# One kernel, a linear attention, an NF4 feed-forward network, an autocorrelation and a linear layer: the autocorrelation's weights transformed at plain delays, its output built from even and odd parts, and the neighbouring linear layer's steps put in another order

## What is computed

```python
x = x + tanh(g_xattn[0]) * linear_attention(layernorm(x), ctx, ctx)
x = x + tanh(g_ffn[0])   * nf4_ffn(layernorm(x), ...)
x = x + tanh(g_xattn[1]) * autocorrelation(layernorm(x), ctx, ctx)
x = x + tanh(g_ffn[1])   * dora_linear(layernorm(x), W, lora_A, lora_B, magnitude)

# autocorrelation, for each batch and channel over the 256 positions t:
corr = ifft(fft(q) * conj(fft(k))).real          # 256 delays
w, idx = top_k(corr, 11); w = softmax(w)
out[t] = sum_i w[i] * v[min(idx[i] + t, 255)]
```

## Time and profile before

| | |
|---|---|
| time, median of 3 runs | 2123.46 us (2122.21 to 2124.3) |
| the profiled execution's own time | 2125.07 us |
| its span in the profile | 2123.3 us |
| TensorE busy | 2036.6 us (96% of the span) |
| VectorE, ScalarE, GpSimd busy | 1098.1, 1175.8, 665.0 us |
| mean granted TensorE clock | 0.986 |
| start of the tail phase's loop | about 1608 us, so some 515 us of the span |

### The profile page before, as it was taken

One profiled execution on the slowest core, in us unless ns is written; L12 is line 12 of the kernel. 1 busy time (PEld: TensorE's weight loads), 2 busy tenths in 40 slices (PEclk: granted clock), 3 DMA queues, 4 the chain that ended last, 5 costly groups with the idle time before them and its releaser, 6 DMA issues. The chain is left out here.

```text
span 2123.3 us, 25966 instructions
## 1 busy us (share of the span) xinstructions
PE 2036.6 (96%) x9634; PEld 1019.5 (48%) x9634; DVE 1098.1 (52%) x1951; ACT 1175.8 (55%) x1851; POOL 665.0 (31%) x640
## 2 busy tenths in 40 slices
PE   6995999999999999999999999999987799999998
PEld 5773444444444444444444444444443455555544
DVE  5775252342624426244262432525257788888872
ACT  6994756656556565565656656565532344434431
POOL 3342211112112121121212112121145666776742
PEclk9997999999999999999999999999998899999999
DMA  6641211112122121211212111111140011111001
GB/s 219 200 143 60 80 50 56 50 50 75 50 68 68 50 75 50 75 61 49 75 50 66 50 56 50 50 56 50 40 148 10 31 40 50 50 36 50 26 21 40
DMA packets 65070, 136.77 MB, mean 64 GB/s; under 512 B 9008, under 2 KB 13744, under 8 KB 64944
## 3 DMA queue, kind: packets, MB, share of 16 engines
q1 hardware_dynamic: 64944, 135.11, 19.5%
HBM read 122.49 MB, written 12.58 MB: 64 GB/s over the span
## 5 line engine op out<-in xcount | busy, mean ns | idle before, releaser
L720 ACT ACTIVATE first<-first 128x512 f32<-128x512 int32 x1008 | 632.7, 628 | 28.0
L904 DVE SCALAR_TENSOR_TENSOR wt<-first,w_scale,absm 128x512 f32<-128x512 f32 x132 | 98.8, 748 | 478.5 <-ACT first L720 477.5
L812 POOL TENSOR_TENSOR gu_lo<-wt,gu_hi 128x512 f16<-128x512 f32 x88 | 102.7, 1167 | 763.5 <-ACT gu_hi L726 763.5
L1053 PE MATMUL a_psQ<-xT_hi,gu_hi 128*128 128x512 f16 x688 | 261.6, 380 | 1.7 <-POOL gu_lo L812 1.7
L1053 PE MATMUL a_psC<-xT_hi,gu_hi 128*128 128x512 f16 x688 | 261.4, 380 | 0.0
L1053 PE MATMUL a_psQ<-xT_lo,gu_hi 128*128 128x512 f16 x688 | 261.3, 380 | 0.0
L1053 PE MATMUL a_psQ<-xT_hi,gu_lo 128*128 128x512 f16 x688 | 261.2, 380 | 0.0
L1053 PE MATMUL a_psC<-xT_lo,gu_hi 128*128 128x512 f16 x688 | 261.2, 380 | 0.0
L1053 PE MATMUL a_psC<-xT_hi,gu_lo 128*128 128x512 f16 x688 | 261.1, 379 | 0.0
L1572 PE MATMUL a_psL<-xT_lo,l_x 128*128 128x512 f16 x768 | 170.5, 379 | 2.5 <-DVE l_x L1644 2.5
L726 ACT ACTIVATE gu_hi<-wt 128x512 f16<-128x512 f32 x88 | 55.1, 626 | 192.6 <-DVE wt L907 192.6
(11 more groups left out here) (277 smaller groups left out, 3829.1 us busy)
## 6 DMA issues: line engine op xcount, KB each, us to landing
first<-in_codes SPq DMA_DIRECT2D x132, 256.0 KB, 2.8
absm<-in_absmax SPq DMA_DIRECT2D x264, 128.0 KB, 3.0
X<-in_x SPq DMA_DIRECT2D x16, 512.0 KB, 4.3
c_in<-in_ctx SPq DMA_DIRECT2D x16, 512.0 KB, 5.4
cT<-in_ctxT SPq DMA_DIRECT2D x16, 512.0 KB, 3.5
xT_hi<-in_ctx SPq DMA_DIRECT2D x8, 1024.0 KB, 7.3
out<-X SPq DMA_DIRECT2D x15, 512.0 KB, 2.6
wide<-in_w SPq DMA_DIRECT2D x8, 512.0 KB, 4.8
```

Of the source, the lines that this page charges most:

```text
L720: act.activation(level[u % 2][:], codes[u % RING] if k == 0 else level[u % 2][:], ACT.Prelu, bias=bias, scale=scale, alpha=alpha).then_inc ...
L812: pool.tensor_tensor(dest(u, 1), wt[u % 2][:], dest(u, 0), ALU.subtract).then_inc(wlo_done, 1)
L904: dve.scalar_tensor_tensor(wt[u % 2][:], source[:], w_scale[:, m:m + 1], absm[u % RING][:], ALU.mult, ALU.mult).then_inc(scaled, 1)
L1053: mm = pe.matmul(o[:], w[c][:, m, k, :], xx[:, k, ts], start=(q == 0), stop=(q == 3 * KD - 1))
```

## The change

The weights are no longer folded before their transpose. `w_fold` on GpSimd is gone; ScalarE scales `cut` itself (four of 256 elements, as many as before), TensorE transposes `cut`, and `weight_even` and `weight_odd` transform all 256 delays with new matrices `delay_hi` and `delay_lo`: twelve float16 products each in place of six. The output is computed as an even part S and an odd part A about the middle of the sequence, 128 positions each: `output` has four float32 products of 512 columns in place of eight, A in psQ[:,1] first, S in psQ[:,0] after it. ScalarE's new `anti_out` copies A to SBUF (128x512), VectorE's `add` adds S to both position tiles (two of 512 elements from psQ[:,0]), and GpSimd's new `anti_add` adds A to the one and subtracts it from the other (two of 128x512), in the next pass. A new `dc_fix` on GpSimd corrects one row of e_d (1x512). Three more constants are loaded: `back`, `delay_hi`, `delay_lo`, while `inv`, `fwd_hi` and `fwd_lo` are halved.

Besides, `q_spectrum(n+2)` now stands ahead of `turn(nxt, 1)`; `linear(d, 0)` starts when half 0 of its tile is ready and waits for half 1 in its middle; VectorE's `low(now, 1)` is in the next pass, behind `products`; and `gain_of(now, 1)` stands behind `add` and `low(nxt, 0)`.

```diff
-                for name in ("fwd", "fwd_hi", "fwd_lo", "inv"):
+                for name in ("fwd", "fwd_hi", "fwd_lo", "inv", "back", "delay_hi", "delay_lo"):
...
-                        pe.wait_ge(res["const_in"], 64)
+                        pe.wait_ge(res["const_in"], 112)
...
-                def w_fold(n):
...
+                def dc_fix(n):
+                    pool.wait_ge(wprod_comb, 4 * n + 1)
+                    pool.tensor_tensor(e_d[0:1, 0, :], e_d[0:1, 0, :], e_d[0:1, 1, :], ALU.subtract).then_inc(dc_done, 1)
+                def anti_add(n):
+                    pool.wait_ge(anti_done, n + 1)
+                    for t, op in enumerate((ALU.add, ALU.subtract)):
+                        pool.wait_ge(sym_done, 2 * n + t + 1)
+                        dst = X[:, 2 * (n // 2) + t, cols(n)]
+                        pool.tensor_tensor(dst, dst, anti[:], op).then_inc(x_done, 1)
...
-                        act.wait_ge(wf_done, 4 * n + 2 * (c // 2) + 2)
-                        act.activation(wf[:, :, c, :], wf[:, :, c, :], ACT.Copy, scale=rws[:, c:c + 1]).then_inc(wn_done, 1)
+                        act.activation(cut[:, c, :], cut[:, c, :], ACT.Copy, scale=rws[:, c:c + 1]).then_inc(wn_done, 1)
+                def anti_out(n):
+                    act.wait_ge(anti_mm, n + 1)
+                    if n:
+                        act.wait_ge(x_done, 2 * n)
+                    act.activation(anti[:], psQ[:, 1, :], ACT.Copy, scale=half_gate[:]).then_inc(anti_done, 1)
...
                 def q_spectrum(n):
                     pe.wait_ge(qlo_done, n + 1)
                     if n >= 2:
-                        pe.wait_ge(x_done, 2 * n - 2)
+                        pe.wait_ge(sym_done, 2 * n - 2)
+                        pe.wait_ge(anti_done, n - 1)
...
+                def weight_spectrum(k):
+                    for half in range(2):
+                        for q, (w, src) in enumerate(((delay_hi, wT_hi), (delay_hi, wT_lo), (delay_lo, wT_hi))):
+                            for h in range(2):
+                                mm = pe.matmul(psE[:, half, :], w[:, 2 * k + half, h, :], src[:, h, :], start=(q + h == 0), stop=(q + h == 3))
+                    mm.then_inc(ws_mm, 1)
...
                 def output(n):
                     pe.wait_ge(prod_done, min(2 * n + 4, 2 * N))
                     pe.wait_ge(wprod_row, n + 1)
-                    for k, src in enumerate((e_d, e_x, n_d, n_x)):
-                        pe.wait_ge(wprod_comb, 4 * n + k + 1)
-                        for t in range(2):
-                            mm = pe.matmul(psQ[:, t, :], inv[:, k, t * P:(t + 1) * P], src[:, 0, :], start=(k == 0), stop=(k == 3))
-                    mm.then_inc(out_mm, 1)
+                    pe.wait_ge(wprod_comb, 4 * n + 2)
+                    pe.matmul(psQ[:, 1, :], back[:, 1, :], e_x[:, 0, :], start=True, stop=False)
+                    pe.wait_ge(wprod_comb, 4 * n + 3)
+                    pe.matmul(psQ[:, 1, :], back[:, 2, :], n_d[:, 0, :], start=False, stop=True).then_inc(anti_mm, 1)
+                    pe.wait_ge(wprod_comb, 4 * n + 4)
+                    pe.matmul(psQ[:, 0, :], back[:, 3, :], n_x[:, 0, :], start=True, stop=False)
+                    pe.wait_ge(dc_done, n + 1)
+                    pe.matmul(psQ[:, 0, :], back[:, 0, :], e_d[:, 0, :], start=False, stop=True).then_inc(out_mm, 1)
...
                 def linear(d, half):
-                    pe.wait_ge(l_lo, 2 * d + 2)
+                    pe.wait_ge(l_lo, 2 * d + 1)
...
+                        if half == 0 and k == KD // 2:
+                            pe.wait_ge(l_lo, 2 * d + 2)
...
-                        dve.scalar_tensor_tensor(dst, psQ[:, t, :], half_gate[:], dst, ALU.mult, ALU.add).then_inc(x_done, 1)
+                        dve.scalar_tensor_tensor(dst, psQ[:, 0, :], half_gate[:], dst, ALU.mult, ALU.add).then_inc(sym_done, 1)
```

More of the change, by code:

```diff
@@ L1176, in spectra @@
     fwd = np.stack([np.cos(even), even_im, np.cos(odd), -np.sin(odd)]).transpose(1, 0, 2)
-    scaled = fwd * DFT_SCALE
-    high = scaled.astype(np.float16)
+    weight = np.where(f == 0, 1.0, 2.0) / L
+    back_im = even_im * weight
+    back_im[:, :1] = np.sin(np.pi * t) / L
+    back = np.stack([np.cos(even) * weight, back_im, np.cos(odd) * 2 / L, -np.sin(odd) * 2 / L]).transpose(2, 0, 1)
     t = np.arange(L)[:, None]
@@ L1181, in spectra @@
     nyquist = np.where(t % 2 == 0, 1.0, -1.0)
-    weight = np.where(f == 0, 1.0, 2.0) / L
     im_inv = -np.sin(even) * weight
     im_inv[:, :1] = (nyquist - 1.0) / L
-    inv = np.stack([np.cos(even) * weight, im_inv, np.cos(odd) * 2 / L, -np.sin(odd) * 2 / L])
-    return fwd.astype(np.float32), high, (scaled - high).astype(np.float16), inv.transpose(2, 0, 1).astype(np.float32)
+    inv = np.stack([np.cos(even) * weight, im_inv]).transpose(2, 0, 1)
+    delay_im = -np.sin(even)
+    delay_im[:, :1] = -nyquist
+    delay = np.stack([np.cos(even), delay_im, np.cos(odd), -np.sin(odd)]).reshape(4, 2, P, P).transpose(2, 0, 1, 3)
+    scaled = [fwd[:, :2] * DFT_SCALE, delay * DFT_SCALE]
+    high = [m.astype(np.float16) for m in scaled]
+    low = [(m - h).astype(np.float16) for m, h in zip(scaled, high)]
+    return {"fwd": fwd.astype(np.float32), "inv": inv.astype(np.float32), "back": back.astype(np.float32),
+            "fwd_hi": high[0], "fwd_lo": low[0], "delay_hi": high[1], "delay_lo": low[1]}
 def phase_tail(nc, io, res):
@@ L1360, in _ @@
                     now = tile(n - LAG)
+                    if 0 < n <= N:
+                        anti_add(n - 1)
                     if n + 1 < N:
@@ L1469, in _ @@
                         odd_out(n + 1)
+                    if n < N:
+                        anti_out(n)
+                    if n + 1 < N:
                         weights(n + 1)
@@ L1729, in _ @@
                         products(n + 1)
+                    if now is not None and n <= N:
+                        low(now, 1)
                     if n < N:
@@ L1750, in _ @@
                         low(nxt, 1)
-                    if now is not None:
-                        gain_of(now, 1)
-                    if nxt is not None and n < N:
-                        low(nxt, 0)
                     if n < N:
@@ L1757, in _ @@
                     if nxt is not None and n < N:
-                        low(nxt, 1)
+                        low(nxt, 0)
+                    if now is not None:
+                        gain_of(now, 1)
                     if n + 3 < N:
```

44 lines of the change are left out of this document (16 added, 28 removed).

## The result

| | before | after |
|---|---|---|
| median of 4 runs | 2123.88 us (2122.21 to 2130.74) | 2162.28 us (2162.22 to 2163.07) |
| ratio | | 1.0177, 95% interval 1.0163 to 1.0191 |
| span of the profiled execution | 2123.3 us | 2160.5 us |
| its mean granted clock | 0.986 | 0.981 |

A forecast was written before the change was run, and what follows sets the result against it. It took TensorE to bound a steady pass, with VectorE's path deciding after the change. 19.5 (passes 3 to 12) + 5.0 + 1.0 = +25.5 us gave 2150.6, or 2149 us against the median; 8-in-10 range 2114 to 2161.

The forecast's parts named there:

- TensorE's sum: Steady pass: output -3.4 us, weights' transforms +2.6, so 28.9 us of TensorE work, 0.85 less than before.
- VectorE's new path: VectorE's steps from W (weight_odd's end): low ends W + 19.4 even, 21.5 odd; passes 30.7 and 32.8 us, +19.5 over ten.
- The rule beside it: Shared port in steady passes: second k_fix would wait the full 1.27 us, not 0.95; 3 us more over ten passes.
- The clock falls too: Rival: on odd passes TensorE's clock falls after idling inside linear, 5 x 1.9 us more, 2158.5; chance 0.17.
- Outside the steady passes: Tail passes other than 3 to 12: together +5.0 and +1.0 us.
- The first pass: Start of the tail: weights start 1.3 us earlier without the fold but have 2.6 more matmul time, +1.3 us.
- Passes 0 to 2: Passes without linear: 29.0 us against 27.65, +1.4 for each of two; masks free, lower clock costing 1.9.
- Pass 14: Pass 14 ends without corr, so its longer weights lie open: +0.9 us.
- The end: Last passes: add(15) comes 3.4 us earlier, but TensorE idles 3.3 for the late statistics: +0.4 us.
- No meetings: Rival: k_fix and offset run undisturbed by GpSimd, every steady pass 29.75 us, about 2125.5; chance 0.10.
- TensorE stays the bound: faster: Rival: low(now, 1) ends by W + 17.7, all passes 28.9 us, about 2114; chance 0.20.
- At no cost: GpSimd's changed list with dc_fix (1.27 us), ScalarE's anti_out (0.6) and the longer constants' transfer add nothing.

The follow-up runs named there:

- g1: Changed kernel with rstd_of ahead of add(now, 1), offset ahead of gain_of, and k_fold and k_fix moved into the next pass; 2126.62 us, ratio 1.0009.
- keep-busy run: Changed kernel with 12 spare float16 matmuls where TensorE idles in the middle of the first linear half, odd passes 3 to 11; 2156.56 us, ratio 1.0148.
- r2: Changed kernel with rstd_of ahead of GpSimd's add(now, 1), and VectorE's k_fix and offset ahead of gain_of(now, 1); 2135.62 us, ratio 1.005.
- r1: Changed kernel with GpSimd's rstd_of ahead of its add(now, 1), nothing else; 2157.16 us, ratio 1.015.
- m1: Changed kernel with its four order moves put back, so the new arithmetic in the order of the kernel before; 2137.75 us, ratio 1.006.
- o1: Kernel before with the change's new order alone, arithmetic as before; 2148.8 us, ratio 1.0113.

## Why the prediction was right or wrong

**TensorE's sum**, 28.9 us: right as a sum. The changed kernel never reaches it, but `g1`'s chain gives it as what is left without the wait.

**VectorE's new path**: right. From W = 1722.40, `add` starts at +11.57 (forecast 11.6) and ends at +12.95 (12.95), `k_fix` starts at +14.06 (14.15), the second one takes 1.65 (0.68 + 0.95), `products` start 4.38 behind K on the odd pass (4.4), and `low` ends at +21.4 (21.5). The even pass lasts 30.73 (30.7). The two meetings are as they were drawn from the earlier trace rows, and `offset` lost its turn, as chosen between the two values.

**The rule beside it**: the Trainium skill, SBUF — State Buffer, section SBUF: two separate sides, gives the shared ports to the instruction that starts first, for the whole of it, and blocks the other until it has ended. In the trace the sum runs from 1736.62 to 1738.27, and `k_fix`, due at 1737.17, ends 0.55 after that: less than its own 0.68, so it waited for nearly all that was left of the sum, which agrees with the rule; but that was only 1.10 us. My use of the rule, the full 1.27 on top, was the error in that sentence; the row's 0.95 was nearer (0.97).

**"The clock falls too"**: wrong chance. It got 0.17 and happened on every odd pass. Against it I had set one row, 2.53 us of idling in pass 15 followed by full speed; the changed kernel has the same 2.53 in pass 15, and its twelve matmuls took 4.46 where twelve at full clock take 2.76. The size, 1.9 a lapse, was near: 1.3 to 1.7 each, 7.5 us over five (the odd passes against 32.83). The keep-busy run shows this for the odd passes. In the tail the miss is 14.7 us (40.2 measured, 25.5 forecast; the stretch ahead of the tail hides 2.9 of it). The ten passes have 7.2 of it, all of it this one choice; the other 7.5 lie outside them.

**"Outside the steady passes"**, forecast 5.0 and 1.0 with pass 0, measured 13.5 in all (the table without its ten passes and its -2.9). Four terms of it were too small.

- *The first pass*, 1.5 short. I counted the fold as a gain and had the masks free; but `k_fold(2)` falls on them. The first two took 1.16 and 1.47 us, where 0.41 is undisturbed, 1.8 us in all, which is more than the 1.3 counted as a gain. The chain of waits at the start of the tail, and the masks of pass 4:

```profile
1611.88 3.27 DVE cut L1732 x8
...
1767.24 1.12 DVE cut L1732 x7
```

- *Passes 0 to 2*, 3.2 short for two, half of it each. The weights' first transform ran at half speed throughout, behind 4.00 us of idling; and the path to it took W + 19.2 in place of 18.5. Most of that is `nmax`, which met GpSimd too (0.98 us where 0.17 is undisturbed), so that `add` ended at W + 12.8 in place of 12.2. The two `k_fix` took 1.38 and 1.65, inside the forecast's "up to 3.3"; its W + 18.5 has room for 2.8 only. The twelve matmuls:

```profile
1650.46 5.20 PE a_psE L1554 x12
```

  The forecast had priced the lapse at 1.9 from the six matmuls and `corr` of before; with twelve matmuls ahead of `corr` it costs 2.6, and `corr` is at full speed again.
- *Pass 14*, 1.7 short: the fallen clock again, 4.46 in place of 2.76. (These are the 2.53 us "in pass 15" of above, which lie ahead of W of pass 15.)
- *The end*, 1.5 short. The prediction does not show how its 3.3 us of idling become +0.4. In the trace TensorE stands twice, 2.19 and 2.79 us, 3.3 more than the 1.67 before; `output` takes 3.4 less; and behind the second stand the eight turns and the 48 matmuls after them take 12.96 us where they took 11.23 before, 1.7 more. Without this last term, the clock once more, the +0.4 would be near.

**"No meetings"** and **"TensorE stays the bound: faster"**: neither took place; their conditions show at `k_fix` (1.65) and at `low`, which ends at W + 19.3 and 21.4 where W + 17.7 was the turning point. The first one's pass of 29.75 us is what `r2`, in which these two meetings are gone, measured: 29.77 and 29.85. The second one needed `select` 0.75 us sooner besides. No kernel here has that: some step of `select` met a GpSimd sum in every steady pass. `g1` has `low` in time, at W + 17.4, and stays at 29.6, but for its pass 3, where `select` ended 0.36 us sooner and the pass is 29.25. So its condition was met nowhere in full, and that it could have been met, by keeping GpSimd off `nmax`, is open.

**"At no cost"**: `dc_fix` took 1.26, as taken; `output` never waited for it. `anti_out` and the longer constants show in no chain.

So the failed steps are two. The clock was taken to hold behind the 3 us of idling in the odd passes, with 0.17 for its fall, and it fell in all five: 7.2 us. And the terms outside the steady passes came to 6.0 where 13.5 was measured, the larger part the fallen clock again, the rest meetings inside `select` that had been put at nothing. What remains open: why the clock fell behind 2.08 us of idling in three passes of `r1` and held in two.

## What to carry to other kernels

Before saving work on the engine that is busy all the time, walk the other engines' serial path between two of its points, and ask on which side of its wait the saving lies: here 3.4 us were saved ahead of the wait and 2.6 added behind it, so a pass of `m1` went from 29.8 to 30.4 us though its matmuls take 0.85 less, and in the new order each further wait on that path was paid in full. Where an instruction releases another engine's sum of two SBUF operands, put the own engine's SBUF work ahead of the release: moving one product behind three short steps returned 21.5 us. And give the fall of the clock behind a new idle stretch of TensorE a price and a fair chance: here stretches of 2 to 3 us inside dense work cost up to 1.7 us beyond their length, though not every time, and one earlier row at full speed was no proof.

## What the runs showed of the hardware that I had not expected

- The clock's fall is not a matter of the length of the stand alone: 0.45 and 0.94 us never, 2.08 in three of five alike passes, 1.98 in four of the five odd passes of `o1`, 3.04 in all five. In pass 14 about 2.5 us ahead of the turn left the clock at 1.00 in the changed kernel and at 0.50 in the keep-busy one. And in `m1` it held behind 4.02 us, where the changed kernel's fell behind 4.00:

```profile
1652.74 0.60 PE L1554 MATMUL a_psE<-xT_hi 128*128 128x512 f16 x2 [4.02 <-DVE wT_lo L1691]
```

  Behind 2.53 us in pass 15 of the changed kernel the first matmuls still ran at full speed before they slowed:

```profile
2102.04 0.60 PE L1554 MATMUL a_psE<-xT_hi 128*128 128x512 f16 x2 [2.53 <-DVE e_x L1745]
2102.48 0.95 PE L1554 MATMUL a_psE<-wT_lo,xT_hi 128*128 128x512 f16 x2
```

- Spare matmuls ahead of a wait made the kernel 5.7 us faster (2156.56 against 2162.28); in the traces the five odd passes are 7.5 us shorter.
- A meeting costs a tiny instruction as much as a large one: two elements a partition took 1.22 us in place of 0.15, where 512 elements took 1.65 in place of 0.69.
- GpSimd's sum over one partition of 512 elements takes 1.26 us, as long as over 128 partitions (1.27).
